# Decay products in row bands 64 apart, and an output projection as native fp32 products

## The reference

```
xz = x @ W_in.T ;  x_in, z = halves of xz
dt = softplus(x @ W_dt.T + b_dt) ;  A = -exp(A_log) * dt
B, C = x @ W_B.T, x @ W_C.T        # 16 heads, state 64
X = x_in * dt                      # 16 heads of 8 features
Y[l] = sum over s <= l of (C[l] . B[s]) * exp(sum of A over s+1..l) * X[s]
y = (Y * silu(z)) @ W_out.T
```

## Time and profile before

| what | us |
|---|---|
| median of 3 runs | 717.67 |
| lowest and highest | 717.45, 719.94 |
| the profiled execution, its own time | 716.94 |
| its span, first to last instruction | 715.0 |
| mamba sections (first decay to last output), within the span | 430.8 to 596.7 |
| the last ffn stream, within the span | 597.5 to 715.0 |
| mean granted TensorE clock | 0.994 |

### The profile page before, as it was taken

The page is one execution under the profiler, slowest core; times in us unless marked ns, Lnnn a source line. Parts: engine busy times, 40 slices in busy tenths (PEclk is TensorE's granted clock), DMA queues, the critical chain, the costliest instruction groups (busy, mean ns, idle before and its releaser), DMA issues. The chain is left out here.

```text
span 715.0 us, 12393 instructions
## 1 busy us (share of the span) xinstructions
PE 673.6 (94%) x4100; PEld 501.8 (70%) x4100; DVE 570.6 (80%) x1311; ACT 417.0 (58%) x756; POOL 323.9 (45%) x404
## 2 busy tenths in 40 slices
PE   7899998697899999999999988999999998999997
PEld 5677774543457777777778776777777775777786
DVE  5899978889978888987989867676766676879775
ACT  4657676885246555556656666555565654455554
POOL 2668873101227766456757543220413200555463
PEclk9999999999999999999999999999999999999999
DMA  6635520000013233222313100000000000323131
GB/s 175 199 102 179 162 86 1 0 1 1 1 49 129 68 113 90 80 69 76 104 54 93 34 1 1 2 3 1 1 2 0 0 2 1 119 75 119 54 125 45
DMA packets 34345, 43.16 MB, mean 60 GB/s; under 512 B 5232, under 2 KB 17520, under 8 KB 34288
## 3 DMA queue, kind: packets, MB, share of 16 engines
q1 hardware_dynamic: 34288, 42.46, 19.6%
HBM read 41.13 MB, written 1.31 MB: 59 GB/s over the span
## 5 line engine op out<-in xcount | busy, mean ns | idle before, releaser
L728 POOL TENSOR_TENSOR p_prod<-p_p,p_gate_row 128x512 f32<-128x512 f32 x128 | 203.6, 1602 | 106.6 <-DVE p_p L524 62.5
L399 ACT ACTIVATE p_sil<-p_ps_a 128x512 f32<-128x512 f32 x176 | 105.1, 597 | 131.8 <-PE p_ps_a L100 127.5
L529 DVE TENSOR_TENSOR p_hlo<-p_prod,p_hhi 128x512 fp32r<-128x512 f32 x176 | 150.0, 854 | 0.3 <-ACT p_hhi L408 0.2
L524 DVE TENSOR_TENSOR p_p<-p_sil,p_ps_b 128x512 f32<-128x512 f32 x128 | 87.2, 681 | 51.9 <-ACT p_sil L399 37.3
L408 ACT CAST p_hhi<-p_prod 128x512 fp32r<-128x512 f32 x176 | 107.9, 615 | 22.4 <-POOL p_prod L728 22.3
L98 PE MATMUL p_ps_a<-xt_hi,w_uphi 128*128 128x512 f32 x176 | 74.2, 422 | 0.0
L98 PE MATMUL p_ps_acc<-p_hhi,w_downhi 128*128 128x512 f32 x176 | 71.1, 404 | 1.2 <-DVE p_hlo L529 1.0
L98 PE MATMUL p_ps_b<-xt_hi,w_uphi 128*128 128x512 f32 x176 | 71.0, 404 | 0.1
L100 PE MATMUL p_ps_a<-xt_hi,w_uplo 128*128 128x512 f32 x176 | 70.1, 398 | 0.0
L99 PE MATMUL p_ps_a<-xt_lo,w_uphi 128*128 128x512 f32 x176 | 70.1, 398 | 0.0
L100 PE MATMUL p_ps_b<-xt_hi,w_uplo 128*128 128x512 f32 x176 | 69.8, 397 | 0.0
(11 more groups left out here) (363 smaller groups left out, 1421.7 us busy)
## 6 DMA issues: line engine op xcount, KB each, us to landing
p_gate_row<-gate_rows SPq DMA_DIRECT2D x128, 256.0 KB, 3.3
w_rawbuf<-in_L_ffn_fc_w_dram SPq DMA_DIRECT2D x3, 512.0 KB, 5.9
w_rawbuf<-in_L_ffn_w_dram SPq DMA_DIRECT2D x3, 512.0 KB, 5.9
w_rawbuf<-in_L_ffn_shared_w_dram SPq DMA_DIRECT2D x3, 256.0 KB, 3.8
out_dram<-x SPq DMA_DIRECT2D x3, 256.0 KB, 3.6
x<-in_L_attn_x_dram SPq DMA_DIRECT2D x2, 256.0 KB, 3.8
x<-in_L_attn_x_dram SPq DMA_DIRECT2D x1, 512.0 KB, 8.3
mb_xraw<-in_L_attn_W_B_dram SPq DMA_DIRECT2D x1, 512.0 KB, 4.9
```

Source lines behind the costliest of these rows:

```text
L399: nc.scalar.activation(sil[:, u % 2], ps_a[:, u % 2], ACT.Silu).then_inc(c["sil"].sem, 1)
L524: nc.vector.tensor_tensor(dst, sil[:, u % 2], ps_b[:, u % 2], ALU.mult).then_inc(c["p1"].sem, 1)
L529: nc.vector.tensor_tensor(hlo[:, u % R], prod[:, u % R], hhi[:, u % R].bitcast(F32), ALU.subtract).then_inc(c["hlo"].sem, 1)
L728: G.tensor_tensor(prod[:, u % R], p1[:, u % 2], gate_row[:, e % ROWS], ALU.mult).then_inc(c["prod"].sem, 1)
```

## The change

Two parts. First, the decay product of token tile t = 1 in quarter q is taken for group q ^ 2 and not for group q, so the two products of a quarter lie in bands whose rows are 64 apart (0 and 64, 32 and 96, and so on). `products(t=1)` and the second part of `outputs` follow that order of groups. Over a section the same work is done. Second, `project_out` takes fp32 operands as they are: `take_y` copies y once in fp32, `low_y` goes, its semaphore goes, and W_out is used raw, so its split goes too. The three passes of fp32r become one native fp32 product for each of the two token tiles.

```diff
+        def group_of(q, t):
+            return q ^ 2 if t else q
...
-                band = slice(32 * q, 32 * q + 32)
                 for t in range(2):
+                    band = slice(32 * group_of(q, t), 32 * group_of(q, t) + 32)
...
-                    hd = head_of(q, k)
+                    hd = head_of(group_of(q, t), k)
...
-                        hd = head_of(q, k)
+                        hd = head_of(group_of(q, part == 1), k)
...
-        self.yT = [sb("mb_yT" + p, [P, SEQ], F32R) for p in ("hi", "lo")]
+        self.yT = sb("mb_yT", [P, SEQ], F32)
...
-        pe.wait_ge(c["m_yl"].sem, c["m_yl"].at(m + 1))
+        pe.wait_ge(c["m_yh"].sem, c["m_yh"].at(m + 1))
         for t in range(2):
-            last = three_pass(pe, bank[:, 2 + t], [q[:, bass.ts(t, P)] for q in self.yT], [q[:] for q in self.w_out], True, True)
+            last = pe.matmul(bank[:, 2 + t], self.yT[:, bass.ts(t, P)], self.w_out, start=True, stop=True)
...
-        self.nc.scalar.copy(self.yT[0][:], bank[:, 0:2].rearrange("p t c -> p (t c)")).then_inc(c["m_yh"].sem, 1)
+        self.nc.scalar.copy(self.yT[:], bank[:, 0:2].rearrange("p t c -> p (t c)")).then_inc(c["m_yh"].sem, 1)
...
-                        if (q, t) == (3, 0) and not more:
-                            tail.low_y(dve, m - 1, ps_y)
...
-                    if q == 3 and not first and more:
-                        tail.low_y(dve, m - 1, ps_y)
...
-            if tail:
-                tail.low_y(dve, -1, last_bank)
...
-        POOL_SPLITS, DVE_SPLITS = {(4, 8): (0, 1, 2), (5, 8): (3,), (6, 8): (4,)}, {}
+        POOL_SPLITS, DVE_SPLITS = {(4, 8): (0, 1), (5, 8): (2,), (6, 8): (3,)}, {}
...
-            tail = MambaTail(keep, nc, counts, x, kept["zs"], mb_w["out"], consts["ident"])
+            tail = MambaTail(keep, nc, counts, x, kept["zs"], mb_raws[2], consts["ident"])
```

More of the change, by code:

```diff
@@ L77, in split_jobs @@
 def split_jobs(sets):
-    return [(job, raw, arrived) for s in sets for job, raw, arrived in zip(s.jobs, s.raws, s.arrived)]
+    return [(job, raw, arrived) for s in sets for job, raw, arrived in zip(s.jobs, s.raws, s.arrived) if job[2] is not None]
 def split_hi(nc, act, c, job):
@@ L1646 @@
 MAMBA_SEMS = ("m_pu m_first m_th m_st m_mom m_c m_rs m_tok m_t m_xh m_xl m_pj m_u m_na m_ex m_ln m_dt m_dA m_dh m_dl m_zs m_sum m_ee "
-              "m_bc m_bh m_mask m_grid m_cut m_rest m_wide m_C m_H m_T m_mv m_D m_cap m_E m_CB m_off m_read m_xp m_xd m_Y m_yc m_sel m_yo m_yb m_yt m_yT m_yh m_yl m_ow "
+              "m_bc m_bh m_mask m_grid m_cut m_rest m_wide m_C m_H m_T m_mv m_D m_cap m_E m_CB m_off m_read m_xp m_xd m_Y m_yc m_sel m_yo m_yb m_yt m_yT m_yh m_ow "
               "m_out m_sl").split()
@@ L1810, in gated @@
         V.tensor_tensor(ytok[:, 1], yo[:], zs[:, seq * 2 + 1], ALU.mult).then_inc(c["m_yt"].sem, 1)
[L1812 to L1816, removed]
     def add_out(self, dve, m, seq, bank):
@@ L2449, in mamba_phase @@
                     "m_xp": 1, "m_xd": 1, "m_Y": 4, "m_yc": 1, "m_sel": 1, "m_yo": 1, "m_yb": 1, "m_yt": 1, "m_yT": 1,
-                    "m_yh": 1, "m_yl": 1, "m_ow": 1, "m_out": 1, "m_th": 1, "m_sl": 1}.items():
+                    "m_yh": 1, "m_ow": 1, "m_out": 1, "m_th": 1, "m_sl": 1}.items():
         c[name].base += k * BATCH
@@ L2535, in program @@
         mb_w = {n: [t[:, a:b] for t in flat] for n, a, b in (("bc", 0, 16 * P), ("in", 16 * P, 18 * P), ("dt", 18 * P, 18 * P + HEADS),
-                                                             ("in_dt", 16 * P, 18 * P + HEADS),
-                                                             ("out", 18 * P + HEADS, 19 * P + HEADS))}
-        places = [mb_w["in"], mb_w["dt"], mb_w["out"]] + [[t[:, 8 * k * P:8 * (k + 1) * P] for t in mb_w["bc"]] for k in range(2)]
+                                                             ("in_dt", 16 * P, 18 * P + HEADS))}
+        places = [mb_w["in"], mb_w["dt"], (None, None)] + [[t[:, 8 * k * P:8 * (k + 1) * P] for t in mb_w["bc"]] for k in range(2)]
         mb.jobs = [(None, parts, *place) for (_, parts, _, _), place in zip(mb.jobs, places)]
```

## The result

| | before | after |
|---|---|---|
| median, us | 718.28 (6 runs beside it) | 713.28 (6 runs, 712.38 to 715.26) |
| ratio, with its 95% interval | | 0.9933 (0.9915 to 0.9952) |
| the profiled execution, its own time | 716.94 | 712.9 |
| its span | 715.0 | 710.9 |
| first decay to the last section's last outputs | 165.02 (430.83 to 595.85) | 161.90 (431.78 to 593.68) |

The change makes the kernel 0.7% faster, just past what the measurement can tell (0.5%). 713.3 was predicted as time and 710.6 as span. Run again, the changed kernel had a stage of 161.97 us and a median of 713.42. One execution of the kernel before, run beside the last two experiments, took 1084.94 us at a mean granted clock of 0.555 and isn't among the ratios.

The account below looks back on a forecast made before the run. TensorE was taken to bind some quarters, the chain over VectorE and ScalarE others. Gains of 2.75 (quarters), 0.55 (last section) and 1.13 (last ffn stream) made 4.4 us: 717.67 to 713.3, range 711.9 to 715.8.

Parts of the forecast that it names:

- The pair: Two decay products of each quarter: the second starts with the first, costing 0.45 us instead of 0.66, 0.213 saved.
- rival 1: Decay products don't overlap: 715.3 us, or 714.0 with loads one behind the other; chance 0.15 for both.
- rival 3: Changing band inside the decay pair costs 0.27 us more for some 20 pairs: 721.5 us; chance 0.04.
- quarter 0, sections 2 to 7, VectorE's part in section 5 included: First products wait for the fourth piece's copy: 0.11 us gained in each of six sections, 0.1 more in section 5.
- quarter 2, sections 1 to 6: The chain over VectorE and ScalarE binds: nothing gained, TensorE's wait ahead of the piece grows from 0.07 to 0.28 us.
- quarter 3, sections 1 to 6: `capped` follows `gated`; the chain allows 0.44 us over sections 3 to 6, and 0.06 in sections 1 and 2.
- section 7 and its end: Quarters 1 and 2 give 0.43 us, quarter 3 nothing; without `low_y` the last outputs start 0.55 earlier.
- last ffn stream: `project_out` starts when `route(1)` frees TensorE, 0.91 us earlier, plus 0.22 by shorter products: 1.13.
- Rival 2: TensorE binds everywhere in the mamba stage: 9.8 us gained in all, 707.9 us; chance 0.04.
- The signs: Expected in the trace: decay records within 0.02 us, next load 0.45 after; both mb_yTlo waits gone, nothing above 0.2 instead.
- Rival 4: Native products in `project_out` cost by array passes, 0.33 us dearer: 713.8 us; chance 0.04.
- rival 5: Clock: last stream's slow stretch, costing 1.4 us, falls away (711.9) or one more comes elsewhere (714.7); chance 0.1.

Follow-up runs that it names:

- The shared copy: Changed kernel with each section's fourth-piece copy split between ScalarE and VectorE: median 713.37 us, ratio 0.9932; split only from section 1 on: 712.88 us, 0.9920.
- the wait kept: Changed kernel with VectorE's subtraction kept, its result unread, and `project_out` waiting for it: median 715.69 us, ratio 0.9967.
- The kernel with four more records: Changed kernel with two heads' products of token tile 1 issued twice in quarters 1 and 2: median 714.55 us (1 run), no ratio.

## Why the prediction came out

**The pair.** Right: both records start within 0.01 us and the pair costs 0.43, not 0.66: 0.23 saved where 0.213 was taken (rival 1 falls). The reason given was too narrow: it argued from halves, since the first products alternate between them, and bands 32 apart in one half do the same (0.43). The Trainium skill (TensorE: Matmul & The Clock Gate, Part 3) speaks of distinct row groups, and the trace agrees. No price of a change of band shows (rival 3 falls).

**Where it counts.** The terms of the sum, against the periods:

| term | predicted | measured |
|---|---|---|
| quarter 0, sections 2 to 7, VectorE's part in section 5 included | 0.76 | 0.57 |
| quarter 1, sections 3 to 6 | 0.85 | 0.94 |
| quarter 2, sections 1 to 6 | 0 | 0.11 |
| quarter 3, sections 1 to 6 | 0.50 | 0.60 |
| section 0 | 0.21 | 0.21 |
| section 7 and its end | 0.43 + 0.55 = 0.98 | 0.69 |
| the mamba stage | 3.30 | 3.12 |
| last ffn stream, `route(1)` to the next product | 1.13 | 1.28 |

Quarters 3 and 0 follow one another over one boundary, and I part what they gain together (1.17 us over six boundaries) by the 0.10 that quarter 3 gains in the kernel with the bands alone. The measured terms are differences of unrounded starts.

**Quarter 0** was mis-sized. The way from the end of `take_bc` to the products was taken as 0.05; it is 0.05 in the unrolled sections and 0.12 in the loop's, so that the slack there was 0.04 and not 0.11. Why it is longer in the loop no run tells. Both parts of the change shared this slack, as the prediction said, but there was little of it to share: alone they shorten the stage by 2.37 and 0.94 us, together by 3.12, so 0.2 is counted twice. The shared copy shows that it was the copy that held the products, since with it quarter 0 gains 0.27 to 0.32 at once in sections 2, 4, 6 and 7 (0.10 in section 3, nothing in section 5, where VectorE is last). In sections 4 and 6 quarter 3 hands 0.1 of it back.

**Quarter 2** behaved as said: the chain over VectorE and ScalarE binds, the wait ahead of the piece is 0.22 in the earlier trace rows's place (0.28 was expected), and 0.23 us more on TensorE doesn't lengthen it. Rival 2, by which TensorE binds everywhere, falls with it, 94% busy or not.

**Section 7** is the term that failed in its step. Quarters 1 and 2 gave 0.23 and 0.24 as said. But quarter 3's `capped` waits for `gated`, and `gated` for quarter 2's `decayed(1)`, which didn't come earlier with the decays of quarter 3. So what quarter 2 gave was taken back there: `capped` starts 2.40 us behind the decays for 2.18 before. The prediction had said that quarter 3 waits for `gated`, and yet counted quarter 2 in full. The kernel with four more records shows the same from the other side: there `capped` starts 2.17 behind the decays, and the section takes over only one of its two added 0.23. The end itself, from that `capped` to the last outputs, fell from 3.84 (592.01 to 595.85) to 3.40 (590.28 to 593.68): 0.44 for 0.55. `decayed(1)` starts 2.66 behind `capped`, right behind the end of exp's second pass (592.91); 2.59 had been taken, and 0.65 for its length, which is 0.69. With the wait kept, this end takes 3.67.

**The signs.** One of them failed by its words: "nothing above 0.2 us" in place of the two waits. TensorE waits 0.54 us for `decayed(1)` in the last section, as the prediction's own times (`project_out` done at 594.75, last outputs at 595.30) imply.

**The last stream** gave 1.28 and not 1.13. From `route(1)`'s last record to the product behind `project_out` it took 1.87 us before (607.31 to 609.18) and takes 0.59 now (604.38 to 604.97). The kernel with the wait kept parts this. Its `project_out` starts 1.15 behind `route(1)`'s last record, as before, and its four records take 0.47, where six took 0.73: 0.26 for the shorter projection, with 0.22 predicted. The rest, 1.02, is the wait: the 0.91 of the prediction, and 0.11 that it left out, since without the wait the first load runs under `route(1)`'s last record.

Rival 4 falls by its price: four native records of 128 columns follow one another by 0.11 like those of fp32r (four loads in 0.53, the last 0.19 long, in the row at 536.77). That doesn't speak against the four passes that the Trainium skill counts for true fp32 (FP8 and Floating Point Precision, TensorE Precision Notes). A native product shows as two records. At 256 columns the records of one half of the rows start 0.21 apart (528.02, 528.23 and 528.45 in the changed kernel's quarter 2), where fp32r records of 256 columns in a piece start 0.12 apart (536.65 and 536.77). So a native record streams about twice as long, and the trace agrees with the page. At 128 columns that would be half of 0.21, no longer than its load (0.11), and so nothing is lost by it; an fp32r record of that size waits for its load all the same.

**Nothing, where nothing was said.** `low_y` in sections 1 to 6: shown by the kernel that keeps it. The dropped split of W_out was not tried alone. In the kernel before it stands at 326.5 (ScalarE) and 328.0 us (GpSimd), and between 310 and 355 us the changed kernel's matmuls stay 0.94 to 0.96 us behind the same matmuls of the kernel before, which leaves no room for a gain or a loss.

**The balance of the spans** is 715.0 - 710.9 = 4.1 us. The stage gives 3.12 and the last stream 1.28, together 4.40 where 4.4 was predicted. The stretch at 1.2 GHz that is absent from the start of the stream gives 0.74: from the last outputs to `project_out` it took 12.60 us before, and 11.86 in the kernel with the bands alone, which has the same order and the same wait there. Against it, the first decay comes 0.95 later (431.78 for 430.83), and 0.1 is left over.

That 0.95 isn't the price of the added stretch of low clock. TensorE's rows, the kernel before, then the changed kernel:

```profile
38.69 0.66 PE L278 MATMUL rw_m<-ident,norm_xn 128*128 128x128 f32 x4 [0.38 <-DVE norm_xn L550]
...
127.27 4.42 PE L1095 MATMUL rw_g<-ident 128*128 128x128 f32 x36 [2.10 <-ACT rw_th L1211]
...
134.46 1.75 PE L1095 MATMUL rw_g<-ident 128*128 128x128 f32 x14 [0.98 <-DVE rw_stat L1415]
```

```profile
39.90 0.65 PE L278 MATMUL rw_m<-ident,norm_xn 128*128 128x128 f32 x4 [0.78 <-DVE norm_xn L550]
...
128.48 5.81 PE L1093 MATMUL rw_g<-ident 128*128 128x128 f32 x36 [2.10 <-ACT rw_th L1209]
...
135.71 1.75 PE L1093 MATMUL rw_g<-ident 128*128 128x128 f32 x14 [0.98 <-DVE rw_stat L1413]
```

The changed kernel is 1.21 us late already at 39.90, and 0.63 of it stands at 18.92 (18.29 before), behind the longer stretch of low clock near the start. In the added stretch its 36 records take 5.81 and not 4.42, but the next group comes 1.25 later and not 2.6: behind those records the kernel before waits 1.12 us for VectorE and the changed kernel doesn't. Some 0.3 of the lateness goes between 212 and 225 us, as it does in every other trace set against that of the kernel before. What made the 0.58 between 19 and 40 us stays open; the change doesn't touch the code there.

So rival 5 was right that a stretch may come or go, and wrong here about its price: 0.74 where it had 1.4, and 0.04 for the one that came. That the span fits (710.9 for 710.6) is partly luck: 0.74 on one side and 0.95 on the other have nothing to do with the sum. So is the time of 713.3: it was counted from the median of 717.67 then known, but beside the changed kernel the kernel before had 718.28, so the medians are 5.0 us apart (3.4 to 6.1 by the interval) and not 4.4. The terms erred by up to 0.3 us to both sides and the errors cancelled as well, so that the sum is nearer than its terms.

## What to carry to other kernels

Price a saving at every place where it recurs, and ask there what comes last once it is gone: of 7.4 us of TensorE time saved in 32 pairs (32 x 0.23), 2.4 arrived. A saving ahead of a wait that hangs on another engine's clock is handed back at that wait, even a quarter later, so follow each saved stretch to the next signal that it doesn't move. To test such a map, add the same time instead of taking it away: the places that don't get longer are those where the saving was lost. And before a slow stretch of one trace is put on the balance, compare the same instructions ahead of it and behind it in both traces: a wait may have swallowed it.

## What the runs showed of the hardware

Two products with 32 rows of contraction and 512 columns, in bands 32 or 64 rows apart, started within 0.01 us of each other, weight loads included; in one band the second came 0.33 later. Records of 128 x 128 x 128 followed each other by 0.11 us in native fp32 (two records a product) as in fp32r. At 256 columns it was 0.21 us in native fp32, with 64 rows, and 0.12 in fp32r. From the end of a ScalarE copy to the waiting weight load it took 0.05 us in unrolled sections and 0.12 in the loop.

The stretches at half clock lie at other places from one trace to the next. All ten traces have one between 9 and 16 us. Others come at 29, 129, 142, 416 or from 709 us on, each in some of the traces only, and the one at 597 us only in that of the kernel before. Their prices differ: 0.74 us at 597, 1.7 at 142 (projection alone, and the changed kernel again), and 0.03 to 0.06 at 129. Lateness can come without them, too: the kernel with the subtraction kept has none between 16 us and its first decay, and that decay comes 2.3 us later than before. Whether the absence at the start of the stream is the change's doing isn't settled: it is absent with either part alone as well, but there is one trace of the kernel before.
